# Grouped attention of layer 2: value mixing done for two key tiles in one visit

## The chip, the cores and the metric

The kernel runs on one core of a Trainium2 chip. The metric is the device time of one execution in microseconds. TensorE is called PE in the rows (PEld is its weight load), VectorE is DVE, ScalarE is ACT, GpSimd is POOL and SyncE, which issues most DMAs, is SP.

## The reference, cut to what matters

The program is four layers, each an attention-like block and a feed-forward block on `x` of 4 x 512 x 512. The change is in the attention of layer 2, which runs over a normalised `x` (queries) and a context (keys and values):

```python
# 32 query heads, 8 key/value heads, 16 wide, 4 query heads (G) to each key head
qh = q.reshape(b, s, KVH, G, D).transpose(0, 2, 3, 1, 4)
scores = jnp.einsum('bkgsd,bktd->bkgst', qh, kh) * scale
attn = jax.nn.softmax(scores, axis=-1)
out = jnp.einsum('bkgst,bktd->bkgsd', attn, vh)
```

## The kernel before

The stage works through 32 groups `n` (`NG`): 4 batches of 8 key heads, each with 4 query heads. A group has 4 steps `tt`, one for each tile of 128 keys. What follows is the order that is written out by hand for each engine; every engine works strictly in its own order.

**Scores for the maximum.** `scores(n + 2, u, j)` (line 1563) is one matmul of 128 queries against 512 keys, for the group two ahead. Two of them (`j` 0 and 1) fill a *unit*, which DVE reduces to a row maximum in `maximum` (line 1743). The units lie in a ring of two, `SU = [BM, BR]`: the first matmul of a unit waits until DVE has freed the unit two before it (`s_free`).

**Scores for the exponential.** `shifted(n, tt, h)` (line 1579) is one matmul of 128 keys against 512 queries of head `h`, with the maximum already taken off. ACT turns it into `PT2[:, tt, h]` (line 1681). These lie in a ring of three banks, `EB`.

**Mixing.** `mix(n, tt)` (line 1589) multiplies the exponentials of one key tile by the values: four matmuls of 128 x 32 weights by 128 x 512, one for each head, each on its own 32 columns of the array and its own 32 partitions of one PSUM bank (`VB`), summed over the four tiles. In the trace they are eight instructions (x8). A mix waits for the exponentials of its tile and hands on `pt_used`.

**Beside these.** `turn_max(n + 1)` (line 1572) follows step `tt` 1, and `turn_out(n - 1)` (line 1596), four transposes of the finished output, follows the mix in step `tt` 2; `turn_out` takes a place in the ring of units, which DVE frees in `finish` (lines 1749 and 1750) after the `maximum` of unit 4 of the group. Some groups have further work, placed in slots by `l2_extra` for PE and ACT and by `beside` for DVE: the norm of a batch (`norm_stats_of`, line 1757, and `norm_rows`, line 1778), `turn_norm` (line 1604), and the routing of the next block, which has `logits` (line 1380).

The units in order on DVE, and what frees their bank:

```python
def maximum(n, u):
    ...
    to = 2 * (u % 2)
    nc.vector.tensor_reduce(NEG2[:, n % 2, u // 2, to:to + 2], unit(("s", n, u))[:, 0:2, :], op=ALU.max, axis=AX.X, negate=True).then_inc(s_free, 1)
```

A slot of `PT2` is used again in the next group. ACT waits for it with this line:

```python
if n:
    act.wait_ge(pt_used, ST * (n - 1) + tt + 1)
```

Before the change, the mix in step `(n, tt)` is that of the tile two steps before; it stands after the second `shifted` and `scores` of the step (`h == 1`), that is, right after the second matmul of a unit. The last two mixes stand back to back at the end of the stage.

Of the kernel before, what the change touches and what calls it, by code (L numbers as in the profile page):

```python
# [15 lines left out]
ST = S // P  # L16
# [76 lines left out]
def flamingo(nc, x, ctx_n, ctx_t, gates, gamma_raw, ident, l0_wq, l0_wk, hadamard, l0_w13, l0_w2, l1_wk, l1_bk, l1_bk_row,  # L93
# [3 lines left out]
    with ctx:  # L97
# [1281 lines left out]
        def route_logit(bank, half, kt):  # L1379
            return nc.tensor.matmul(bank[0:E, :], RW[:, kt, :], XT[:, half, kt, :], start=kt == 0, stop=kt == KT - 1)  # L1380

        def turn_logits(bank):
            for st in range(ST):
                last = nc.tensor.transpose(bank[:, st * E:(st + 1) * E], LT[:, st * P:(st + 1) * P], ID[64:64 + E, 64:64 + E])
            return last

        def route_ranks(bank):
            n = ST * E
            ohs = OHS.rearrange("p t e -> p (t e)")
            nc.tensor.matmul(bank[:, 0:n], TRI, ohs, start=True, stop=True)  # L1390
            return nc.tensor.matmul(bank[:, n:2 * n], ONE, ohs, start=True, stop=True)
# [47 lines left out]
        def l2_extra(n, tt):  # L1439

            b, g = divmod(n, KVH)
            jobs = []
            if b < B - 1 and (g, tt) in N_SLOTS:
                jobs.append(("n", b, N_SLOTS.index((g, tt))))
            if b and (g, tt) in Q_SLOTS:
                jobs.append(("q", b - 1, Q_SLOTS.index((g, tt))))
            if b and (g, tt) in R_SLOTS:
                jobs.append((("lg", "lt", "rk")[R_SLOTS.index((g, tt))], b - 1))
            return jobs
# [90 lines left out]
        def l2_tensor(pe):  # L1540
            pe.wait_ge(turn.free, T_PE.now() + 2)
            pe.wait_ge(rows_in, 8 * 16)

            def evict(job):
                pe.wait_ge(e_free, L2[job] + 1)
                return EB[L2[job] % 3]

            def unit(job):
                pe.wait_ge(s_free, L2[job] + 1)
                return SU[L2[job] % 2]  # L1550

            def scores(n, u, j):
                b, g = divmod(n, KVH)
                if u == 0 and j == 0:
                    half = g // 4
                    if g % 4 == 0:
                        pe.wait_ge(q_in[half], 64 * (b + 1))
                        pe.wait_ge(k_in[half], 64 * (b + 1))
                    pe.wait_ge(q_zero, n + 1)
                if j == 0:  # L1560
                    pe.wait_ge(s_free, L2["s", n, u] + 1)
                st = 2 * (u % 2) + j
                last = nc.tensor.matmul(SU[L2["s", n, u] % 2][:, j, :], QS2[0:KR, 4 * g + u // 2, st * P:(st + 1) * P], KS2[0:KR, g, :], start=True, stop=True)  # L1563
                if j == 1:
                    last.then_inc(s_full, 1)

            def turn_max(n):
                pe.wait_ge(l2_const, 3)
                pe.wait_ge(nm_ready, n + 1)
                bank = evict(("m", n))  # L1570
                for st in range(ST):
                    last = nc.tensor.transpose(bank[0:8, st * P:(st + 1) * P], NM[:, st, :], ID[:, :])
                last.then_inc(e_full, 1)

            def shifted(n, tt, h):
                g = n % KVH
                if tt == 0 and h == 0:
                    pe.wait_ge(qm_in[n % 2], 32 * (n // 2 + 1))
                nc.tensor.matmul(evict(("e", n, tt, h)), KS2[0:KR, g, tt * P:(tt + 1) * P], QS2[0:KR, 4 * g + h, :], start=True, stop=True)\  # L1579
                  .then_inc(e_full, 1)  # L1580

            def mix(n, tt):
                if tt == 0:
                    pe.wait_ge(v_staged, n + 1)
                    if n:
                        pe.wait_ge(out_copied, n)
                pe.wait_ge(e_free, L2["e", n, tt, G4 - 1] + 4)
                for h in range(G4):
                    last = nc.tensor.matmul(VB[32 * h:32 * h + 32, :], VW[:, tt, n % KVH, :], PT2[:, tt, h, :], start=tt == 0, stop=tt == ST - 1)  # L1589
                last.then_inc(pt_used, 1)  # L1590

            def turn_out(n):
                pe.wait_ge(out_copied, n + 1)
                bank = unit(("o", n))[:, 0, :]
                for st in range(ST):
                    last = nc.tensor.transpose(bank[:, st * P:(st + 1) * P], OUT2[:, st * P:(st + 1) * P], ID[:, :])
                last.then_inc(s_full, 1)

            def turn_norm(job, b, kt):
                if kt == 0:  # L1600
                    pe.wait_ge(xn_ready, N_PE.step())
                bank = evict((job, b, kt))
                for st in range(ST):
                    last = nc.tensor.transpose(bank[:, st * P:(st + 1) * P], XN[:, st, kt * P:(kt + 1) * P], ID[:, :])
                last.then_inc(e_full, 1)

            def logits(b):
                bank = evict(("lg", b))
                pe.wait_ge(l2_in, 80)
                pe.wait_ge(e_free, L2["q", b, KT - 1] + 4)  # L1610
                for kt in range(KT):
                    last = route_logit(bank, (b + 1) % 2, kt)
                last.then_inc(e_full, 1)

            def back(b):
                bank = evict(("lt", b))
                pe.wait_ge(lt_ready, b + 1)
                turn_logits(bank).then_inc(e_full, 1)

            def ranks(b):  # L1620
                bank = evict(("rk", b))
                pe.wait_ge(ones_ready, 1)
                pe.wait_ge(ohs_ready, b + 1)
                route_ranks(bank).then_inc(e_full, 1)

            for n in range(2):
                for u in range(8):
                    for j in range(2):
                        scores(n, u, j)
            turn_max(0)  # L1630
            for n in range(NG):
                for tt in range(ST):
                    for h in range(G4):
                        shifted(n, tt, h)
                        if n + 2 < NG:
                            scores(n + 2, 2 * tt + h // 2, h % 2)
                        if h == 1 and ST * n + tt > 1:
                            mix(*divmod(ST * n + tt - 2, ST))
                        if tt == 2 and h == 1 and n:
                            turn_out(n - 1)  # L1640
                    if tt == 1 and n + 1 < NG:
                        turn_max(n + 1)
                    for job in l2_extra(n, tt):
                        if job[0] in "nq":
                            turn_norm(*job)
                        if job[0] == "lg":
                            logits(job[1])
                        if job[0] == "lt":
                            back(job[1])
                        if job[0] == "rk":  # L1650
                            ranks(job[1])
            for tt in range(ST - 2, ST):
                mix(NG - 1, tt)
            turn_out(NG - 1)
# [1377 lines left out]
        @block.tensor  # L3032
        def _(pe):
            l0_tensor(pe)
            l1f_tensor(pe)
            l2_tensor(pe)
            moe_tensor_tiles(pe, *moe_tensor(pe))
            l3_tensor(pe)
            l3f_tensor(pe)
# [138 lines left out]
```

## Time and profile before

| | us |
|---|---|
| median of 3 runs | 3797.08 |
| lowest and highest | 3795.95, 3798.74 |
| the profiled execution, its own time | 3797.58 |
| its span | 3795.8 |
| attention of layer 2, steady part of the span | 1080 to 1530 |

The profiled execution lies 0.5 us over the median, and 1.8 us of it outside the span. In the rows a time is a start in us from the beginning of the span, and the number behind it the busy time. A bracket tells how long the engine sat idle before and who ended that.

### The profile page before, as it was taken

What the parts mean: (1) busy time and instruction counts of PE and PEld (TensorE: products, weight loads), DVE (VectorE), ACT (ScalarE), POOL (GpSimd) and SP (SyncE); (2) the same over time, 40 slices, a digit from 0 to 9 for tenths busy, and PEclk for the clock granted to TensorE, in tenths of its full rate; (3) what the DMA queues carried; (4) which work ended last, traced back from release to release, by engine and by line L of the source; (5) the groups of instructions that cost most, each with busy time, mean ns of one, the idle gap of its engine ahead of it and who ended that gap; (6) DMA issues with size and microseconds to landing.
All of it is one profiled execution on the core that took longest, in us unless ns stands there. A gap on an engine that the chain in (4) does not pass through costs nothing.

```text
span 3795.8 us, 38099 instructions
## 1 busy us (share of the span) xinstructions
PE 3552.7 (94%) x12973; PEld 1916.1 (50%) x12974; DVE 2174.4 (57%) x3831; ACT 1406.2 (37%) x2908; POOL 627.8 (17%) x588
## 2 busy tenths in 40 slices
PE   5999999996889999599959999999999999999999
PEld 1444444442445444366524444444444445888888
DVE  7656666235678777311137665656565665655554
ACT  7524343111357667222223444444343443111111
POOL 5100000000132331211111100000000002544543
PEclk7999999998989999799979999999999999999999
DMA  7321312210422323555542100010101002111220
GB/s 235 133 74 67 128 63 71 111 45 26 95 64 57 90 63 86 182 163 160 162 155 71 48 27 36 25 38 25 38 25 38 25 26 89 67 67 45 78 78 23
DMA packets 81846, 294.03 MB, mean 77 GB/s; under 512 B 17928, under 2 KB 18824, under 8 KB 66832
## 3 DMA queue, kind: packets, MB, share of 16 engines
q1 hardware_dynamic: 74304, 269.32, 21.8%
q0 software_dynamic: 7376, 22.57, 1.9%
q8 instruction: 96, 1.57, 0.2%
q14 instruction: 70, 0.57, 0.0%
HBM read 248.31 MB, written 38.81 MB: 76 GB/s over the span
## 4 chain that ended last, share of the span: by engine, by line
PE 85%; DVE 9%; POOL 2%; DMA 2%; ACT 2%; issue 1%; SPq 0%; DVEq 0%; ACTq 0%; POOLq 0%
PE BM L2316 6%; PE BM L2376 6%; PE BM L444 5%; PE BR L444 5%; PE BR L2387 4%; PE BM L2751 3%; PE BS L2751 3%; PE BR L2751 3%; PE BS L460 3%; PE BT L460 3%; PE BT L2368 3%; PE BT L1589 3%; PE BR L2021 3%; PE BM L2329 3%; PE BM L2010 3%; PE BR L2010 2%
## 5 line engine op out<-in xcount | busy, mean ns | idle before, releaser
L2447 ACT COPY AR<-BM 128x512 f32<-128x512 f32 x320 | 187.5, 586 | 409.6 <-PE BM L2329 122.1
L2556 DVE SCALAR_TENSOR_TENSOR X<-BR,AR,X 128x512 f32<-128x512 f32 x256 | 189.0, 749 | 208.5 <-PE BR L2387 199.9
L228 POOL TENSOR_TENSOR RSTD<-VAR,HALF 128x4 f32<-128x4 f32 x32 | 34.6, 1081 | 1451.9 <-DVE VAR L2572 925.5
L2387 PE MATMUL BR<-AR 128*128 128x512 f32 x512 | 253.7, 618 | 12.7 <-DVE X L2556 11.3
L2376 PE MATMUL BM<-AR 128*128 128x512 f32 x512 | 246.4, 593 | 0.0
L444 PE MATMUL BM<-XT,AR 128*128 128x512 f32 x512 | 230.6, 593 | 0.9 <-ACT AR L598 0.9
L2316 PE MATMUL BM<-XT,AR 128*128 128x512 f32 x512 | 229.9, 602 | 0.7 <-ACT XT L241 0.7
L444 PE MATMUL BR<-XT,AR 128*128 128x512 f32 x512 | 230.2, 592 | 0.0
L1681 ACT ACTIVATE PT<-BS 128x512 f32<-128x512 f32 x340 | 191.9, 596 | 73.4 <-PE BS L1579 68.2
L605 ACT ACTIVATE AR<-AR 128x512 f32<-128x512 f32 x256 | 182.5, 714 | 83.3 <-DVE AR L733 79.7
L2543 DVE TENSOR_REDUCE AR<-BS 128x2 f32<-128x1024 f32 x64 | 78.5, 1227 | 215.9 <-PE BS L2356 215.9
L2368 PEld LDWEIGHTS BT<-ID,AR 128*128 128x128 f32 x1024 | 127.3, 140 | 137.6 <-issue 133.3
L710 DVE TENSOR_SCALAR_CACHE_REDUCE AR<-AR 128x512 f32<-128x512 f32 x264 | 186.3, 743 | 3.5
L1743 DVE TENSOR_REDUCE NEG<-BM 128x2 f32<-128x1024 f32 x129 | 157.6, 1222 | 49.6 <-PE BM L1563 47.8
L2459 ACT COPY AR<-BT 128x512 f32<-128x512 f32 x256 | 150.9, 589 | 84.0 <-PE BT L2368 83.7
L2387 PEld LDWEIGHTS BR<-AR 128*128 128x128 f32 x512 | 85.7, 188 | 177.9 <-DVE X L2556 93.8
L2453 ACT ACTIVATE AR<-BS,AR 128x512 f32<-128x512 f32 x128 | 86.9, 683 | 237.1 <-DVE AR L2543 237.1
L1743 DVE TENSOR_REDUCE NEG<-BR 128x2 f32<-128x1024 f32 x127 | 155.0, 1221 | 30.4 <-PE BR L1563 27.8
L2316 PEld LDWEIGHTS BM<-XT,AR 128*128 128x128 f32 x512 | 95.3, 191 | 132.6 <-issue 131.6
L444 PEld LDWEIGHTS BR<-XT,AR 128*128 128x128 f32 x512 | 97.3, 190 | 122.5 <-issue 122.5
L444 PEld LDWEIGHTS BM<-XT,AR 128*128 128x128 f32 x512 | 96.6, 190 | 123.5 <-issue 123.5
L2368 PE MATMUL BT<-ID,AR 128*128 128x128 f32 x1024 | 153.6, 272 | 2.7 <-ACT AR L2453 2.7
(447 smaller groups left out, 6914.4 us busy)
## 6 DMA issues: line engine op xcount, KB each, us to landing
AR<-l_wq_dram SPq DMA_DIRECT2D x32, 1152.0 KB, 5.1
AR<-l_w_dram SPq DMA_DIRECT2D x36, 1024.0 KB, 4.9
AR<-l_w_dram SPq DMA_DIRECT2D x64, 512.0 KB, 3.3
AR<-l_w_dram SPq DMA_DIRECT2D x42, 768.0 KB, 4.8
AR<-w2h SPq DMA_DIRECT2D x16, 1024.0 KB, 4.8
QS<-qx SPq DMA_DIRECT2D x32, 512.0 KB, 9.5
AR<-l_w_dram SPq DMA_DIRECT2D x8, 1408.0 KB, 8.4
made<-AR SPq DMA_DIRECT2D x40, 256.0 KB, 4.8
```

Of the source, the lines that this page charges most:

```text
L444: last = nc.tensor.matmul(bank, w[:, kt, a, :], XT[:, b & 1, kt, :], start=kt == 0, stop=kt == KT - 1)
L460: last = nc.tensor.matmul(S_BANKS[st], f.HIDDEN[:, u, st * P:(st + 1) * P], f.DOWN[:, u, :], start=u == 0, stop=u == UG - 1)
L1681: nc.scalar.activation(PT2[:, tt, h, :], evict(("e", n, tt, h)), ACT.Exp, scale=float(HD ** -0.5)).then_inc(e_free, 1)
L1743: nc.vector.tensor_reduce(NEG2[:, n % 2, u // 2, to:to + 2], unit(("s", n, u))[:, 0:2, :], op=ALU.max, axis=AX.X, negate=True).then_inc(s_ ...
L2010: last = nc.tensor.matmul(bank[:, 0:I].rearrange("p (a n) -> p a n", a=1), XGT[:, u, kt * P:(kt + 1) * P], EW1[:, ds(e * KT + kt, 1), c:c ...
L2316: last = nc.tensor.matmul(bank, WS[:, p % 2, at:at + P], XT[:, b % 2, kt, :], start=kt == 0, stop=kt == KT - 1)
L2368: last = nc.tensor.transpose(BT[:, L3[job] % 2, st * P:(st + 1) * P], PROB3[h][:, st, lt * P:(lt + 1) * P], ID[:, :])
L2376: last = nc.tensor.matmul(BM[:, L3[job] % 2, :], KVN[:, p // 8 * ST + lt, :], PROBT3[:, lt, :], start=lt == 0, stop=lt == ST - 1)
L2387: nc.tensor.matmul(BR[:, L3[job] % 2, :], CC3[h][:, st * P:(st + 1) * P], W3[:, p % 8 * 2 + h, :], start=True, stop=True)\
L2447: nc.scalar.copy(to, BM[:, L3[job] % 2, :]).then_inc(m_free, 1)
L2556: nc.vector.scalar_tensor_tensor(out=xb, in0=BR[:, L3[job] % 2, :], scalar=RS3[:, p % 2, h, st:st + 1], in1=xb, op0=ALU.mult, op1=ALU.add) ...
L2751: last = nc.tensor.matmul(bank[:, unit * HALF_N:(unit + 1) * HALF_N], left[k][:, unit, kt * P:(kt + 1) * P], right[k][:, kt, :], start=kt ...
```

## The change

Mixes no longer come one to a step. Steps with an odd `tt` have two, back to back, for the tiles three and two steps before; steps with an even `tt` have none. The pair stands where the single one stood. Group `n` is then mixed in step `(n, 3)` (its tiles 0 and 1) and in step `(n + 1, 1)` (its tiles 2 and 3). The last two mixes of the stage are as before.

```diff
-                        if h == 1 and ST * n + tt > 1:
-                            mix(*divmod(ST * n + tt - 2, ST))
+                        if h == 1 and tt % 2 == 1 and ST * n + tt > 1:
+                            for t in range(2):
+                                mix(*divmod(ST * n + tt - 3 + t, ST))
                         if tt == 2 and h == 1 and n:
                             turn_out(n - 1)
```

## Rows read from the trace of the kernel before

**Rows 1.** Busy time by stretch: window, length, engines, granted clock, DMA share, GB/s.

```profile
1080.00:1530.00 450.00, 437.15 (x2385) 224.17 (x2384) 347.79 (x451) 321.25 (x611) 133.38 (x181) 1.00 0.26 68
```

**Rows 2.** Waits in 1080 to 1530: who waited for whom, total, times, longest.

```profile
PEld BM L1563 <- DVE NEG L1743: 9.1, 12, 1.0
```

**Rows 3.** Timeline of PE over four mixes in groups without other work.

```profile
1154.68 1.06 PE L1589 MATMUL BT<-PT,VW 128*32 128x512 f32 x8
1155.67 0.50 PE L1579 MATMUL BS<-QS,KS 128*128 128x512 f32 x1
1156.01 0.39 PE L1563 MATMUL BM<-KS,QS 128*128 128x512 f32 x1
...
1157.40 0.39 PE L1563 MATMUL BR<-KS,QS 128*128 128x512 f32 x1
1157.72 1.06 PE L1589 MATMUL BT<-PT,VW 128*32 128x512 f32 x8
1158.71 0.50 PE L1579 MATMUL BT<-QS,KS 128*128 128x512 f32 x1
...
1161.19 1.06 PE L1589 MATMUL BT<-PT,VW 128*32 128x512 f32 x8
...
1164.62 1.06 PE L1589 MATMUL BT<-PT,VW 128*32 128x512 f32 x8
```

**Rows 4.** Timeline of DVE over the same groups.

```profile
1156.91 1.23 DVE L1743 TENSOR_REDUCE NEG<-BM 128x2 f32<-128x1024 f32 x1 [0.68 <-PE BM L1563]
1158.05 1.21 DVE L1743 TENSOR_REDUCE NEG<-BR 128x2 f32<-128x1024 f32 x1
...
1161.30 1.22 DVE L1743 TENSOR_REDUCE NEG<-BR 128x2 f32<-128x1024 f32 x1
...
1163.17 0.42 DVE L1750 TENSOR_TENSOR TMP<-BM,RS 128x256 f32<-128x256 f32 x1
```

**Rows 5.** Timeline of ACT over the same groups: two exponentials.

```profile
1156.21 0.60 ACT L1681 ACTIVATE PT<-BS 128x512 f32<-128x512 f32 x1 [0.96 <-PE BS L1579]
1156.70 0.59 ACT L1681 ACTIVATE PT<-BT 128x512 f32<-128x512 f32 x1
```

**Rows 6.** Timeline at the end of the stage: two mixes back to back.

```profile
1527.25 2.08 PE L1589 MATMUL BT<-PT,VW 128*32 128x512 f32 x16
```

**Rows 7.** The same place, short windows: second half of the first mix, second mix's weights.

```profile
1527.71 0.61 PE L1589 MATMUL BT<-PT,VW 128*32 128x512 f32 x4
...
1528.27 0.16 PEld L1589 LDWEIGHTS BT<-PT,VW 128*32 128x32 f32 x8 [0.86 <-ACT PT L1681]
```

**Rows 8.** Timeline of all engines where a unit's bank is freed late.

```profile
1201.83 1.22 DVE L1743 TENSOR_REDUCE NEG<-BM 128x2 f32<-128x1024 f32 x1
...
1203.11 0.50 PE L1563 MATMUL BM<-KS,QS 128*128 128x512 f32 x1 [0.28 <-DVE NEG L1743]
1203.44 0.39 PE L1579 MATMUL BT<-QS,KS 128*128 128x512 f32 x1
```

**Rows 9.** Timeline of PE in groups 8 and 9, where DVE has the norm: mixes.

```profile
1183.68 1.07 PE L1589 MATMUL BT<-PT,VW 128*32 128x512 f32 x8
...
1190.72 1.06 PE L1589 MATMUL BT<-PT,VW 128*32 128x512 f32 x8
...
1197.47 1.06 PE L1589 MATMUL BT<-PT,VW 128*32 128x512 f32 x8
...
1205.35 1.06 PE L1589 MATMUL BT<-PT,VW 128*32 128x512 f32 x8
```

**Rows 10.** Timeline of DVE in group 8: the norm's statistics among the units.

```profile
1187.05 0.68 DVE L1757 BATCH_NORM_STATS2 STAT<-X 128x6 f32<-128x512 f32 x1
1187.65 1.21 DVE L1743 TENSOR_REDUCE NEG<-BR 128x2 f32<-128x1024 f32 x1
...
1194.09 0.68 DVE L1757 BATCH_NORM_STATS2 STAT<-X 128x6 f32<-128x512 f32 x1
...
1195.30 1.23 DVE L1743 TENSOR_REDUCE NEG<-BM 128x2 f32<-128x1024 f32 x1
```

## The prediction

> **What bounds the kernel now.** I read the attention stage alone, since nothing else in the program is touched. First the busy time by stretch: between 1080 and 1530 us PE is busy 437 us of 450 at a granted clock of 1.00, DVE 348 and ACT 321 [rows 1]. PE looks like the bound; but DVE works 77% of the time, so it has 0.8 us of idle time to a step and no more. Then the waits: for DVE to free the bank BM the weight loads of `scores` waited only a dozen times, 9.1 us in all [rows 2]. So the ring of two units is just deep enough today. Last the timelines, which show how the three engines mesh.
>
> In a step without other work, PE needs 3.04 us from mix to mix (1154.68 to 1157.72). The mix holds PE for 0.99 us, from 1154.68 to the next `shifted` at 1155.67; the second matmul after that starts 0.34 later, the following ones every 0.23 ((1157.40 - 1156.01) / 6), and the next mix 0.32 after the last of them [rows 3]. On DVE the first unit after a mix starts 1.24 us after that `shifted` (1156.91), the next one 1.14 later, and each takes 1.22 to its end [rows 4].
>
> **What the change removes.** 126 mixes become 63 visits of two, so 63 entries and exits. Against the plain spacing of 0.23, a mix costs 3.04 - 8 x 0.23 = 1.20 us [rows 3]. What does the second mix of a visit cost? The end of the stage has such a pair: 16 instructions take 2.08 us, where eight take 1.06 [rows 3, 6]. That is 1.02, but the second one's weights had waited for ACT there [rows 7], so 1.02 is the upper bound. Within a mix, its second half starts 0.46 after the first (1527.25 to 1527.71) [rows 6, 7]; two such halves give 0.92, which I take, and I take it as the lower bound too, as nothing in the rows shows two halves closer together. So a visit of two saves 1.20 - 0.92 = 0.28 us (0.18 at the upper bound) on PE, 63 x 0.28 = 17.6 us if nothing else moved. From mix start to the next `shifted` a double visit takes 0.99 + 0.92 = 1.91 us.
>
> The Trainium skill, TensorEngine Tiling (Array Packing), Key Properties, says that changing the tiling mode drains the array, and a mix is such a change. The trace agrees with a small price: the entry is 0.32 instead of 0.23 and the first spacing behind it 0.34 [rows 3]. By the page alone fewer switches would be a gain, and that is the faster rival below.
>
> **What it moves.** Nothing is added: no instruction, no DMA, no queue passed over. But PE now leaves the scores for 1.91 us at a time, and between visits it must issue four units and eight `shifted` instead of two and four. DVE cannot store up that much, since the ring holds two units. I follow one stretch from the first `shifted` after a visit (time 0) to the next. B, C, D, E are its units; a bank freed late releases the matmul after 0.06 us, and the next one starts 0.33 behind it, not 0.23 (1203.11 to 1203.44). The 0.06 is 1203.11 against the end of the unit before it, 1201.83 + 1.22 [rows 8].
>
> *Stretch from step (n,3) to (n+1,1), no other work.* B starts on DVE at 1.24 and ends at 2.46; C starts at 2.38 and ends at 3.60. D needs B's bank: its turn on PE comes at 0.34 + 8 x 0.23 = 2.18, but it starts at 2.52; its second matmul is at 3.08. E's turn is at 3.54, but C's bank is free only at 3.60: start 3.66, second matmul 4.22, visit at 4.54, end 4.54 + 1.91 = 6.45. Today two steps take 6.08 [rows 3]. So **+0.37**, though the visit itself saved 0.28: the stalls and their restarts cost 0.65. DVE ends E at 5.9 to 6.0 and starts the next unit at 7.69, so 1.7 us idle in each stretch.
>
> *Stretch from (n,1) to (n,3), no other work.* `turn_max` pushes C on DVE to 1161.30 - 1158.71 = 2.59, its end to 3.81 [rows 3, 4]. `turn_out` takes the bank of B, so D needs C's: start 3.87 where its turn was 3.2, second matmul 4.43. DVE's `finish`, whose larger instruction takes 0.42 [rows 4], ends by my estimate about 4.6, before E's turn at 4.89, and E follows freely: second matmul 5.35, visit 5.67, end 7.58. Today 6.90 (1157.72 to 1164.62) [rows 3]. So **+0.68**.
>
> *Stretches in which DVE has other work.* Two are followed in group 8, where the norm's statistics stand behind the odd units, each 0.60 us (1187.05 to 1187.65), the last with its small followers 1.21 (1194.09 to 1195.30) [rows 10]. From (8,1): C starts at 2.99, ends at 4.20, D starts on PE at 4.26, second matmul at 4.82, E's at 5.74, visit 6.06, end 7.97; today 7.04 (1183.68 to 1190.72): **+0.93**. From (8,3): C starts 3.60 and ends 4.82, which holds E until 4.88, its second matmul 5.44, visit 5.76, end 7.67; today 6.75 (1190.72 to 1197.47): **+0.92** [rows 9]. But the next stretch already takes 7.88 (1197.47 to 1205.35) [rows 9], partly because DVE and ACT are behind; work that DVE still has at the visit covers part of the longer gap, so there I expect less than half. Over such stretches I take +0.6 each, with 0 and 0.93 as ends.
>
> *Why ACT is not the next bound.* Exponentials that are ready follow at 0.49 us (1156.21 to 1156.70) [rows 5]; eight make 4.0 of a stretch of 6.45. No slot of `PT2` comes late: ACT's `exps(n, 0)` and `exps(n, 1)` need mixes of step (n-1, 3), `exps(n, 2)` and `exps(n, 3)` those of (n, 1), which PE issues before the `shifted` of these tiles. ACT's copy of the output comes after the same mix as today, and SP and POOL wait for nothing that moves, other than by the stage's own length.
>
> **The sum.** 62 stretches lie between the 63 visits. Counted in the trace, 10 of the first kind are free of other work (6.06 to 6.09 us, as in rows 3) and 9 of the second (6.90 to 6.92): 10 x 0.37 + 9 x 0.68 = 9.8 us. Three hold the logits of the routing, for which PE waits over 2 us anyway, and in four at the end no scores are left: 0. The other 36 at 0.6 make 21.6. Together +31.4. The profiled execution's 3797.6 becomes 3829.0; the median of the runs lies 0.5 below it, so 3828.5 us, +0.8%.
>
> **Rivals.**
> *Faster: PE's time is all that counts.* The saving of 17.6 us arrives, 3779.5 us. For it: PE busy 437 of 450. Against it: the ring. It decides where DVE frees C's bank before E's undelayed turn: a unit would have to take about 0.9 us instead of 1.14 to 1.22. This is also the drain rule's case. The Trainium skill's page gives no figure for a drain here. 6%.
> *No change:* only the 19 plain stretches lose (+9.8), and the other 36, where DVE is behind anyway, give back 0.28 each, -10.1: 3797 us. For it: stretches of 7.88. Against it: the two stretches of group 8 come out clearly longer. 6%.
> *Slower by much more:* stalls of ACT's ring of three banks come on top, as ACT too starts empty after a visit. If each of the 58 stretches with scores pays 1.1: +64, 3861 us. For it: ACT copies of norm and output bunch up in the same stretches. Against it: ACT's 0.49 cadence. 12%.
> *My forecast* has the rest, 76%.
>
> **Range.** Lower end: the plain stretches alone, +9.8, 3807. Upper end: all 36 others at 0.93 (33.5) with the 9.8, and 1.02 for the second mix (62 x 0.10 = 6.2): +49.5, 3847. That leaves the three rivals outside, about 2 in 10. A change of under 0.2% (7.6 us) cannot be told from none here. Slower has the forecast and the last rival, 0.88; same 0.06; faster 0.06.
>
> **What the profile after would show.** 63 visits of x16 beside the one at the end, 1.98 to 2.08 us each. Plain stretches of 6.45 and 7.58. `scores` (line 1563) waiting for DVE in nearly every stretch, some 30 us in all instead of 9. DVE idle for PE in each stretch about 1.7 us at a time. The stage about 31 us longer, the granted clock still 1.00, all else as it was. I would be wrong if the double visit took less than about 1.5 us (then a plain stretch breaks even), or if PE found free banks after a visit.

## The result and the profile after

The changed kernel takes 3822.69 us (median of 4 runs, 3822.08 to 3825.62) against 3797.91 us before (4 runs, 3795.95 to 3799.02). The ratio is 1.0067, 95% interval 1.005 to 1.0085. It is slower by 24.8 us; the forecast was 3828.5, so +31. The profiled execution took 3825.62 us with a span of 3823.8. Three single executions below (one each of the kernel before, of the old order with the norm's work moved, and of one with a pair in step (n,3)) ran at a lower granted clock and took 5150 to 7090 us; all comparisons leave them out.

The busy time by stretch, with the columns of [rows 1]:

```profile
1080.00:1560.00 480.00, 443.18 (x2396) 232.09 (x2394) 347.80 (x456) 321.43 (x613) 134.97 (x182) 1.00 0.25 64
```

DVE and ACT do what they did in [rows 1] (347.8 and 321.4 us of work), PE is busy for 443 us of 480 and its granted clock is still 1.00. So no work was added; the same work lies more apart.

The waits in 1080 to 1560 (who waited for whom, total, times, longest):

```profile
PEld BM L1563 <- DVE NEG L1744: 29.8, 37, 1.6
PEld BR L1563 <- DVE NEG L1744: 22.9, 33, 1.7
PE BM L1563 <- DVE NEG L1744: 17.1, 30, 1.2
PE BR L1563 <- DVE NEG L1744: 11.0, 24, 1.4
```

For the bank BM, the weights of `scores` wait 29.8 us instead of 9.1 [rows 2], and those for BR wait 22.9 instead of 2.2. On the matmuls, the wait for DVE is 17.1 + 11.0 = 28.1 us, where it was 7.7 + 1.0 = 8.7 before. The forecast of some 30 us instead of 9 holds for BM's row and for the matmuls; it had left BR out. The two kinds of rows are two views of one wait and aren't added.

The timeline of PE over the stretch from step (5,3) to (6,1), with no other work, to be laid beside [rows 3]:

```profile
1158.24 1.92 PE L1589 MATMUL BT<-PT,VW 128*32 128x512 f32 x16
1160.10 0.51 PE L1579 MATMUL BS<-QS,KS 128*128 128x512 f32 x1
1160.44 0.40 PE L1563 MATMUL BM<-KS,QS 128*128 128x512 f32 x1
...
1162.63 0.50 PE L1563 MATMUL BM<-KS,QS 128*128 128x512 f32 x1 [0.16 <-DVE NEG L1744]
1162.96 0.40 PE L1579 MATMUL BT<-QS,KS 128*128 128x512 f32 x1
1163.20 0.39 PE L1563 MATMUL BM<-KS,QS 128*128 128x512 f32 x1
...
1163.75 0.19 PEld L1563 LDWEIGHTS BR<-KS,QS 128*128 128x128 f32 x1 [0.36 <-DVE NEG L1744]
1163.76 0.51 PE L1563 MATMUL BR<-KS,QS 128*128 128x512 f32 x1
1164.10 0.40 PE L1579 MATMUL BS<-QS,KS 128*128 128x512 f32 x1
1164.34 0.40 PE L1563 MATMUL BR<-KS,QS 128*128 128x512 f32 x1
1164.66 1.92 PE L1589 MATMUL BT<-PT,VW 128*32 128x512 f32 x16
1166.52 0.50 PE L1579 MATMUL BT<-QS,KS 128*128 128x512 f32 x1
```

and DVE in the same stretch, beside [rows 4]:

```profile
1158.57 1.22 DVE L1744 TENSOR_REDUCE NEG<-BR 128x2 f32<-128x1024 f32 x1
1161.35 1.23 DVE L1744 TENSOR_REDUCE NEG<-BM 128x2 f32<-128x1024 f32 x1 [1.56 <-PE BM L1563]
1162.49 1.22 DVE L1744 TENSOR_REDUCE NEG<-BR 128x2 f32<-128x1024 f32 x1
1163.62 1.23 DVE L1744 TENSOR_REDUCE NEG<-BM 128x2 f32<-128x1024 f32 x1
1164.77 1.23 DVE L1744 TENSOR_REDUCE NEG<-BR 128x2 f32<-128x1024 f32 x1
1167.74 1.23 DVE L1744 TENSOR_REDUCE NEG<-BM 128x2 f32<-128x1024 f32 x1 [1.75 <-PE BM L1563]
```

Take 1160.10 as time 0. Unit D's first matmul starts at 2.53, E's at 3.66, E's second at 4.24, the visit at 4.56 and the next stretch at 6.42. The two stalls are visible: D's matmul and E's weights are released by DVE, and the next matmul follows 0.33 and 0.34 behind. DVE is busy for four units and then idle 1.75 us, until the first unit after the visit is there.

From the mix starts of the two timelines I took all 62 stretches of both kernels:

| kind of stretch | count | before | after | sum of differences, us |
|---|---|---|---|---|
| (n,3) to (n+1,1), plain | 10 | 6.07 to 6.08 | 6.40 to 6.42 | +3.4 |
| (n,1) to (n,3), plain | 9 | 6.90 to 6.92 | 7.51 to 7.54 | +5.6 |
| with the logits of the routing | 3 | 10.35 to 10.37 | 10.14 to 10.15 | -0.7 |
| at the end, few or no scores | 4 | 5.21 to 6.55 | 5.43 to 6.79 | 0.0 |
| the others | 36 | 6.75 to 8.34 | 6.63 to 8.96 | +16.0 |
| all | 62 | 442.4 | 466.8 | +24.4 |

The first double visit comes 1.3 us later than the mix it replaces, but that is no loss of the change: the stage's first `shifted` already starts 1.5 us later (1073.95 for 1072.42), before any mix. Behind the last double visit 0.9 us are lost. From the first `shifted` to the last mix the stage takes 25.0 us longer, and the medians differ by 24.8.

### The profile page after: what moved, and what is told of

It reads as the page before. It is cut to its first block, busy times and chain, and to the rows that moved or that the text cites. A ratio compares the mean times of both kernels' runs of the same rounds, so it can differ in the third digit from the quotient of the medians.

```text
span 3823.8 us, 38099 instructions
## 1 busy us (share of the span) xinstructions
PE 3557.2 (93%) x12973; PEld 1925.1 (50%) x12974; DVE 2171.1 (57%) x3831; ACT 1404.0 (37%) x2908; POOL 627.5 (16%) x588
## 4 chain that ended last, share of the span: by engine, by line
PE 84%; DVE 9%; POOL 2%; DMA 2%; ACT 2%; issue 1%; SPq 0%; DVEq 0%; ACTq 0%; POOLq 0%
PE BM L2317 6%; PE BM L2377 6%; PE BM L444 5%; PE BR L444 5%; PE BR L2388 4%; PE BM L2752 3%; PE BR L2752 3%; PE BS L2752 3%; PE BT L1589 3%; PE BS L460 3%; PE BT L460 3%; PE BT L2369 3%; PE BR L2022 3%; PE BM L2330 3%; DVE NEG L1744 3%; PE BM L2011 2%
```

## The experiments

**Shorter reduces.** If DVE's pace against a ring of two units makes the loss, a DVE of twice the speed must turn it into the gain of 0.34 us a visit. The edit was made to both kernels:

```diff
-nc.vector.tensor_reduce(..., unit(("s", n, u))[:, 0:2, :], op=ALU.max, axis=AX.X, negate=True)
+nc.vector.tensor_reduce(..., unit(("s", n, u))[:, 0:2, 0:256], op=ALU.max, axis=AX.X, negate=True)
```

> The kernel before, but each row maximum looks at only the first 256 of its 512 keys, so a reduce reads 128x512 instead of 128x1024 (the part of the computation that is changed; the shift of the exponential is then not the true maximum). This is the base for the same edit to the changed kernel. Both theories: plain stretches stay at 6.08 and 6.90 us, since PE sets them; the stretches with norm and routing on DVE get shorter, 5 to 20 us in all.

> The changed kernel with the same shorter reduces (row maxima over the first 256 keys only). Theory (the ring of two units and the speed of DVE set the stretch): with DVE twice as fast no bank comes late, plain stretches are 6.08 - 0.34 = 5.74 and 6.90 - 0.34 = 6.56 us, and the kernel is about 21 us (63 x 0.34) faster than the kernel before with the same edit. Rival (the double visit itself costs PE more, by a drain, late weights or late exponentials, or ACT's ring binds): the stretches stay above 6.08 and 6.90 and the pair of kernels keeps a loss of 10 us or more.

Measured: 3784.59 us with the old order and 3786.41 with the new one (ratios to the kernel before 0.9964, interval 0.9952 to 0.9977, and 0.9967, 0.9954 to 0.9979). The loss is gone, but the gain of 21 us isn't there. By stretches the theory is half right. The plain stretch from (n,3) to (n+1,1) took 5.73 to 5.79 us, as it said. The plain (n,1) to (n,3) only went from 7.53 down to between 7.00 and 7.06, where 6.56 was forecast, against 6.90 with the old order; (9,3) to (10,1) stayed at 7.54 (6.97 with the old order). Something else than DVE's speed holds these.

**A ring of four single banks.** Same PSUM, same result, but each `scores` matmul signals by itself, DVE reduces bank by bank and frees bank by bank (the indices and counts that go with it are left out here):

```diff
-        SU = [BM, BR]
+        SU = [BM[:, 0, :], BM[:, 1, :], BR[:, 0, :], BR[:, 1, :]]
...
-                nc.vector.tensor_reduce(NEG2[:, n % 2, u // 2, to:to + 2], unit(("s", n, u))[:, 0:2, :], op=ALU.max, axis=AX.X, negate=True).then_inc(s_free, 1)
+                for j in range(2):
+                    nc.vector.tensor_reduce(NEG2[:, n % 2, u // 2, to + j:to + j + 1], unit(("s", n, u, j)), op=ALU.max, axis=AX.X, negate=True).then_inc(s_free, 1)
```

> The kernel before with the ring of two units of two banks made a ring of four single banks: every scores matmul has its own signal, DVE reduces 128x512 twice where it reduced 128x1024 once. Same PSUM, same result. Theory: plain stretches are set by PE and stay at 6.08 and 6.90; DVE pays some 0.05 to 0.1 us more per unit (256 units), which shows only where DVE is behind: -5 to +10 us in all.

> The changed kernel with the ring of four single banks. Theory (the coarse ring makes the loss): DVE starts on the first bank at 0.77 us instead of 1.24 and frees banks every 0.6; the bank that a matmul needs is then always free, and a plain stretch takes PE's own 5.74 and about 6.6 to 6.77 us. The loss turns into a gain of 5 to 20 us against the kernel before. Rival (DVE has too little work stored at a visit whatever the grain, since the same four banks hold it): plain stretches stay above 6.08 and the kernel is slower than before by 10 us or more.

Measured: 3791.35 us with the old order (0.9980, 0.9970 to 0.9989) and 3789.77 with the new one (0.9976, 0.9967 to 0.9986). Of the changed kernel's 24.8 us all are gone, and both versions beat the kernel before. Between the two orders there is no difference beyond the intervals, so in the finer ring merging the mixes costs or wins nothing that can be told. Plain stretches of the new order took 5.72 to 5.78 us (5.74 forecast) and 6.85 to 7.03. The timeline of DVE in the fine ring, around the mix that starts at 1137.31 (the next starts at 1143.03):

```profile
1136.33 1.29 DVE L1743 TENSOR_REDUCE NEG<-BR 128x1 f32<-128x512 f32 x2
1137.54 1.28 DVE L1743 TENSOR_REDUCE NEG<-BM 128x1 f32<-128x512 f32 x2
1139.93 1.29 DVE L1743 TENSOR_REDUCE NEG<-BR 128x1 f32<-128x512 f32 x2 [1.12 <-PE BR L1563]
1141.14 1.28 DVE L1743 TENSOR_REDUCE NEG<-BM 128x1 f32<-128x512 f32 x2
1142.34 1.28 DVE L1743 TENSOR_REDUCE NEG<-BR 128x1 f32<-128x512 f32 x2
```

DVE starts sooner after the visit and is idle 1.12 us instead of 1.75, though two halves cost 1.20 us where one unit costs 1.14. The rival of that run, that four banks hold the same work whatever the grain, is out.

**The same two mixes, apart.** Here the two mixes of an odd step have half a step between them, so no visit is long:

```diff
-                        if h == 1 and tt % 2 == 1 and ST * n + tt > 1:
-                            for t in range(2):
-                                mix(*divmod(ST * n + tt - 3 + t, ST))
+                        if h % 2 == 1 and tt % 2 == 1 and ST * n + tt > 1:
+                            mix(*divmod(ST * n + tt - 3 + h // 2, ST))
```

> The changed kernel with its two mixes in the same odd steps, but two matmuls of a unit and two shifted ones between them (one at the second, one at the fourth place of the step). Each visit is then single and short. Theory (units come unevenly to a ring of two): after the second visit three units follow with no mix between them; the third waits for the first one's bank, C starts on DVE at 3.35, E's first matmul at 4.63, and the plain stretch takes 6.50 us, the kernel stays about as slow as the changed one, +15 to +30 us over the kernel before. Rival (only the length of one absence of PE counts, or only its lateness): plain stretches near 6.08 us, the kernel within 5 us of the kernel before.

Measured: 3822.58 us (1.0064, 1.0047 to 1.0081), as slow as the changed kernel, and plain stretches of 6.58 to 6.61 us, 0.1 over the forecast. Short visits don't help: it is enough that three units in a row must pass a ring of two without a mix between them. The third one's bank comes late, here in the stretch whose first mix starts at 1157.34:

```profile
1163.04 0.50 PE L1563 MATMUL BR<-KS,QS 128*128 128x512 f32 x1 [0.23 <-DVE NEG L1743]
```

Over PE's own pace this order loses 6.59 - 6.08 = 0.51 us in a stretch, the changed kernel with its long visit 6.41 - 5.74 = 0.67, so cutting the visit in two takes little of the loss away.

**ACT's copies.** The stretches that neither shorter reduces nor the fine ring brought to PE's pace have copies on ACT. Both orders, in the fine ring, were run with these copies cut to 64 of their 512 columns:

```diff
-                nc.scalar.copy(OUT2[:, :], VB).then_inc(out_copied, 1)
+                w = 64 if n else S
+                nc.scalar.copy(OUT2[:, 0:w], VB[:, 0:w]).then_inc(out_copied, 1)
...
-                nc.scalar.copy(XT[:, (b + 1) % 2, kt, :], bank)
-                nc.scalar.copy(QHL[:, 0, kt, :], bank).then_inc(q_hi, 1)
+                nc.scalar.copy(XT[:, (b + 1) % 2, kt, 0:64], bank[:, 0:64])
+                nc.scalar.copy(QHL[:, 0, kt, 0:64], bank[:, 0:64]).then_inc(q_hi, 1)
```

> The kernel before with the ring of four banks, and ACT's copies of the output (from the second group on) and of the norm cut to their first 64 of 512 columns, so that the rest of those tiles keeps older values (the part of the computation that is left out). Base for the same edit to the changed kernel; only the stretches between mixes are read. Both theories: plain stretches 6.08 and 6.90 us, as PE sets them.

> The changed kernel with the ring of four banks and the same cut of ACT's copies. With the ring of four banks alone the plain stretch from (n,1) to (n,3) took 6.86 to 7.02 us where PE alone would need 6.56, and the stretch (9,3) to (10,1) 7.54 against 6.97 before. Theory (ACT's copies behind a double visit, against its ring of three banks, are what is left there): the first falls to 6.55 to 6.77, the second to 6.6 to 7.1. Rival (units of DVE or PE itself): both stay within 0.1 us.

Measured: with the old order the plain stretches stayed at 6.08 and 6.90 and (9,3) to (10,1) at 6.97. With the new one the plain (n,1) to (n,3) fell to 6.62 to 6.64 us, from 6.85 to 7.03 in the fine ring, and (9,3) to (10,1) from 7.55 to 6.81. Totals 3789.57 us (6 runs) and 3779.45 (2 runs; 0.9975, 0.9963 to 0.9986, and 0.9950, 0.9930 to 0.9970). So with both out of the way the new order is faster than the old one: by 10 us in the medians, of which one rests on two runs, and by 7.9 us in the sum of the 62 stretches (424.5 for 432.4). Two mixes of the fine ring with whole copies, then of the one with short copies, both from step (n,1) to (n,3):

```profile
1155.65 1.92 PE L1587 MATMUL BT<-PT,VW 128*32 128x512 f32 x16
...
1162.67 1.92 PE L1587 MATMUL BT<-PT,VW 128*32 128x512 f32 x16
```

```profile
1154.93 1.92 PE L1587 MATMUL BT<-PT,VW 128*32 128x512 f32 x16
...
1161.57 1.92 PE L1587 MATMUL BT<-PT,VW 128*32 128x512 f32 x16
```

7.02 and 6.64 us; one copy of the output takes 0.59 us whole and 0.22 cut, which is about the difference. In the first of the two stretches PE's `shifted` waits for the exponential that has its bank:

```profile
1159.01 0.59 ACT L1674 COPY OUT<-BT 128x512 f32<-128x512 f32 x1
1161.02 0.19 PEld L1577 LDWEIGHTS BT<-QS,KS 128*128 128x128 f32 x1 [0.43 <-ACT PT L1680]
1161.51 0.19 PEld L1577 LDWEIGHTS BS<-QS,KS 128*128 128x128 f32 x1 [0.19 <-ACT PT L1680]
```

So ACT's ring of three banks is a second bound behind a double visit. ACT too comes out of the visit empty, and what it then has to do besides exponentials comes late.

**The norm's work moved into DVE's gap.** The statistics and rows on DVE were put behind the units before a visit (shown for the statistics of one kind):

```diff
-                if g == 0 and b < B - 1 and late:
-                    norm_stats_of(b + 1, st)
+                two = {2: (0, 1), 6: (2, 3)}.get(slot, ())
+                if g == 0 and b < B - 1:
+                    for s in two:
+                        norm_stats_of(b + 1, s)
```

> The changed kernel with the norm's statistics and rows on DVE moved to stand behind the units just before a visit (behind units 2 and 6 instead of the odd units or one behind each). Theory (DVE is idle for 1.7 us at every visit and busy between): statistics disappear into that gap; stretches of 7.63 and 7.90 go towards 6.4 and 7.5. In all 6 to 12 us faster than the changed kernel. Rival (these stretches are long for PE's or ACT's sake): no change beyond 2 us.

> The same move of the norm's work in the kernel before. Theory: DVE's gap at a single visit is 0.6 us and two pieces of 0.6 no longer fit into one gap, so nothing is won or some lost: -2 to +6 us. If it gained as much as in the changed kernel, the move would have nothing to do with the double visits.

> The changed kernel with both, the ring of four banks and the norm's work behind the units before a visit. Theory: the two add up, as the one takes the stalls out of the plain stretches and the other out of those with norm work: 10 to 25 us faster than the kernel before, the fastest of all. Rival: the finer ring has already taken the stalls out and the move adds nothing.

Measured: 3818.94 us with the changed order (1.0057, 1.0040 to 1.0074), 3.8 less than the changed kernel where 6 to 12 were forecast; 3808.90 with the old order (1.0025, 1.0012 to 1.0037), 10 more than before where -2 to +6 were forecast; 3792.67 with the fine ring (0.9984, 0.9974 to 0.9994), 3 more than the fine ring alone where the two should add up. The stretches with statistics did what was forecast (7.63 fell to 6.39 to 6.58, 7.90 to 7.54). But the move also put two norm rows of groups 11, 19 and 27 behind unit 6, and in groups 11 and 19 they cost several us: (11,3) to (12,1) took 12.80 us with the old order instead of 6.97, and 8.82 with the new one instead of 6.82. The timeline of all engines in the old order shows how:

```profile
1235.64 2.51 POOL L1871 TENSOR_TENSOR QHL<-XT,QHL 128x512 fp32r<-128x512 f32 x2
...
1236.89 3.56 DVE L1778 TENSOR_SCALAR XN<-X,MV,RSTD 128x512 f32<-128x512 f32 x2
...
1238.21 1.96 POOL L1853 MEMSET QS<- 2x2048 f32 x1
1240.38 1.21 DVE L1743 TENSOR_REDUCE NEG<-BM 128x2 f32<-128x1024 f32 x1
1240.52 1.12 PE L1604 MATMUL BS<-ID,XN 128*128 128x128 f32 x4 [2.86 <-DVE XN L1778]
```

That failure says nothing about double visits; it is told under the last heading.

**One pair to a group.** In the fine ring, with the remaining mixes single, the pair was tried in either place:

```diff
-                        if h == 1 and ST * n + tt > 1:
+                        if h == 1 and tt != 0 and ST * n + tt > 1:
+                            if tt == 1:
+                                mix(*divmod(ST * n + tt - 3, ST))
                             mix(*divmod(ST * n + tt - 2, ST))
```

(the other has `tt != 2` and `tt == 3`.)

> The kernel before with the ring of four banks, and only one pair of mixes to a group: tiles 2 and 3 of the last group in step (n,1), tiles 0 and 1 singly in steps (n,2) and (n,3), none in step (n,0). Theory: after the single visit at (n,3) DVE and ACT have no output copy to do and four units without a mix pass at PE's own pace, 0.99 + 3.88 = 4.87 us; the other half takes 6.90 + 0.86 = 7.76. A plain group is then 12.63 us instead of 12.98, the kernel 3 to 9 us faster than the same ring with the old order. Rival: the double visit still starves ACT before its two copies, the second half takes 8.0 or more and nothing is won.

> The same with the pair in the other place: tiles 0 and 1 in step (n,3), tiles 2 and 3 of the last group singly in (n,0) and (n,1), none in (n,2). Theory: the stretch without a mix now holds ACT's two copies and turn_out, so ACT's ring of three banks delays it by some 0.3 us and eats the saving: plain group 12.9 to 13.0 us, the kernel within 3 us of the same ring with the old order. If fine_pair1 and this one came out the same, ACT's copies would not be what is left.

Measured: 3790.87 us (0.9981, 0.9971 to 0.9990) and 3792.45 (0.9980, 0.9970 to 0.9990), against 3791.35 for the fine ring with the old order. The plain group took 12.64 us with the pair in step (n,1), as forecast, and 12.92 to 13.11 with the pair in (n,3). But the first gained only 0.5 us in all where 3 to 9 were forecast: in groups where DVE has the norm, the two steps without a mix took 6.28 to 6.30 us instead of the plain 4.88, so what the plain groups win is lost there. No placing of pairs beat the fine ring alone by more than the measurement can tell.

## Why the prediction was right

**The mechanism and the plain stretches.** They came out as computed: 6.41 for 6.45, 7.53 for 7.58, DVE idle 1.75 us for 1.7, D's and E's first matmuls at 2.53 and 3.66 for 2.52 and 3.66. In the other kind, D's and E's first matmuls came at 3.86 and 4.90 for 3.87 and 4.89. Nearly all of the error in both is the second mix, 0.05 us. The shorter reduces, the fine ring and the mixes put apart each moved the shorter kind of plain stretch within 0.1 us of where the ring theory put it. That the coarse ring makes the loss there is shown. It is not the only cause in every stretch: (9,3) to (10,1) keeps its loss of 0.57 us with either edit to DVE and gives it up with short copies on ACT.

**The cost of the second mix** was taken too high. A visit takes 1.85 to 1.86 us from its start to the next `shifted` (1164.66 to 1166.52), so the second mix costs 0.87, not 0.92. The first half of a mix is followed by the next 0.46 later, but the later halves are 0.43 apart, as the weights of the visit that starts at 1158.24 show:

```profile
1158.70 0.13 PEld L1589 LDWEIGHTS BT<-PT,VW 128*32 128x32 f32 x4 [0.30 <-issue]
1159.13 0.13 PEld L1589 LDWEIGHTS BT<-PT,VW 128*32 128x32 f32 x4 [0.30 <-issue]
```

I had doubled the 0.46 and called 0.92 the lower bound because nothing in the rows showed less. Sixteen instructions take 1.92 us where weights don't wait, and not the 2.08 of [rows 6], which had the wait of [rows 7] in it. Over the 19 plain stretches this is 1.0 us. The stretches' sum was forecast 7.0 us too high (31.4 for 24.4); 0.8 of this lies in the plain stretches, 5.6 in the next term and 0.7 in those with the logits.

**The 36 other stretches** were put at +0.6 each, 21.6 us; they came to +0.44, 16.0 us. The 0.6 was a guess between 0 and 0.93 and not worked out, so how near this term came is luck in part. The two that I had followed were near (7.90 for 7.97, 7.63 for 7.67). What I had not followed were seven stretches (n,3) to (n+1,1) in which DVE has routing work or norm rows behind it or in it (n = 11, 13, 14, 19, 21, 22 and 27): they got shorter by 0.15 to 1.12 us, 4.2 us in all. The other 29 came to +0.70 each, above the 0.6. In group 13 the cause can be read. Before, DVE's routing burst lies after the mix at 1266.51 and holds PE afterwards:

```profile
1267.51 0.49 PE L1579 MATMUL BT<-QS,KS 128*128 128x512 f32 x1
1268.69 0.50 PE L1563 MATMUL BM<-KS,QS 128*128 128x512 f32 x1 [0.69 <-DVE NEG L1743]
```

After the change the same burst and the unit behind it run while PE is on its double visit, and PE finds its bank:

```profile
1281.20 1.92 PE L1589 MATMUL BT<-PT,VW 128*32 128x512 f32 x16
1283.06 0.50 PE L1579 MATMUL BT<-QS,KS 128*128 128x512 f32 x1
1283.39 0.40 PE L1563 MATMUL BM<-KS,QS 128*128 128x512 f32 x1
```

On DVE the unit behind the burst holds the bank that PE's first `scores` needs. In the old order it ends at 1268.63, 1.1 us after PE is back at 1267.51; in the new one it ends at 1283.13, and that matmul starts on time at 1283.39:

```profile
1267.41 1.22 DVE L1743 TENSOR_REDUCE NEG<-BM 128x2 f32<-128x1024 f32 x1
```

```profile
1281.90 1.23 DVE L1744 TENSOR_REDUCE NEG<-BM 128x2 f32<-128x1024 f32 x1
```

A long visit costs where DVE is caught up and pays back where DVE is behind. For the other six stretches this is only argued.

**ACT is not the next bound** was right for the changed kernel's plain stretches, where DVE is later still. It was wrong as a general statement: take the ring of units away as a bound, and ACT's copies hold the stretch at 6.85 to 7.03 instead of 6.62, and they are what keeps (9,3) to (10,1) at 7.54 with either edit to DVE. The rival of ACT's ring had that mechanism, but not its price. In the fine ring cutting the copies took 10 us off the new order and 2 to 3 off the old one, and 1.0 us at most off one stretch; the rival had 1.1 in each of 58.

**The logits and the end** were put at 0 and are -0.7 and 0.0. The first 0 was near for a wrong reason. In the stretches with the logits PE doesn't wait for over 2 us: it is busy with the logits, and it is DVE that sits idle, so no bank comes late and part of the visit's saving arrives (10.14 for 10.36). The kernel before shows it:

```profile
1251.36 3.60 PE L1380 MATMUL BS<-XT,AR 128*8 128x512 f32 x8
1256.19 1.23 DVE L1743 TENSOR_REDUCE NEG<-BM 128x2 f32<-128x1024 f32 x1 [3.49 <-PE BM L1563]
```

The 0.0 of the four at the end is the sum of -0.61, +0.59, +0.21 and -0.18, which is luck. The 0.9 us behind the last double visit were not in the sum at all.

**The faster rival** has a small true core: the plain 5.74 us is what PE alone makes of a pair, and with the fine ring the kernel shows it. With short copies on ACT as well, 8 to 10 us reach the total. What speaks for the double visit by the Trainium skill, TensorEngine Tiling (Array Packing), Key Properties, fewer changes of the mode, is worth 1.20 - 0.87 = 0.33 us each here. It pays for a change of the ring, not for itself.

## What to carry to other kernels

When an engine's absences are merged, ask not how long it is away but how much its consumers can hold: here a ring of two units bridged one mix and no more, and a saving of 0.33 us a visit turned into a loss of 0.34 or 0.62 a stretch. Work the ring through once by hand, from the first unit after the absence to the next absence; four rows of each engine were enough to be within 0.05 us. Before giving a ring more memory, give it a finer grain: four single banks in place of two pairs, in the same PSUM, took 7.7 us off the old order and all of the loss off the new one. Then look for the next ring: here ACT's, which kept the merged mixes from winning anything.

## What the runs showed of the hardware that was not expected

**DVE rows that wait inside the instruction.** A norm row (`tensor_scalar`, 128x512) took 0.54 us in other groups. In the moved version two of them in group 11 took 3.56 us from 1236.89 on, and no wait is recorded for DVE. Taken one by one:

```profile
1236.89 1.54 DVE L1778 TENSOR_SCALAR XN<-X,MV,RSTD 128x512 f32<-128x512 f32 x1
1238.36 2.10 DVE L1778 TENSOR_SCALAR XN<-X,MV,RSTD 128x512 f32<-128x512 f32 x1
```

The first ends 0.28 us after GpSimd's `tensor_tensor` (1238.15), the second 0.29 after its `memset` (1240.17). In group 27 of the same run the same two rows stand behind the same unit, but GpSimd has no such work, as it has no queries to prepare for another batch. There they took 0.54 us each, and the stretch 7.50 us instead of 7.03:

```profile
1481.13 0.99 DVE L1778 TENSOR_SCALAR XN<-X,MV,RSTD 128x512 f32<-128x512 f32 x2
```

With the new order the picture is the same (1.32 and 2.11 us in group 11, 0.54 each in group 27). The reduce beside GpSimd's `tensor_tensor` (from 1235.76), which reads PSUM, kept its 1.22 us. The Trainium skill, SBUF — State Buffer, in its section on the two separate sides, says that a DVE instruction in a 2-port mode and a GpSimd one take a shared pair of ports as an exclusive lock, and that the later one is blocked until the other is done. The trace agrees with it; the mode in which the rows ran is not shown in it.

**The clock after it.** PE then had nothing to do for 2.86 us and its granted clock fell from 1.00 to 0.50, which is 1.2 GHz. Busy time by stretch, with the columns of [rows 1]:

```profile
1230.00:1238.00 8.00, 7.66 (x43) 3.98 (x42) 7.29 (x9) 6.18 (x12) 3.51 (x4) 1.00 0.01 2
1238.00:1240.50 2.50, 0.00 (x0) 0.00 (x0) 2.50 (x3) 0.07 (x1) 2.12 (x2) 0.84 0.57 209
1240.50:1245.60 5.10, 5.08 (x17) 2.58 (x18) 2.31 (x2) 1.68 (x3) 0.44 (x2) 0.50 0.84 310
```

So 3 us of waiting became 5.8 us in the stretch (12.80 for 6.97). With the new order the same rows left PE without work for 1.79 us, and the granted clock stayed at 1.00 (8.82 for 6.82), though the DMA share behind it was as high (0.92). In the changed kernel itself PE never sits idle for more than 1.4 us from 1080 to the last mix, and the granted clock of that stretch is 1.00.
